# Cross-attention on a context taken relative to its last token: one subtraction in place of the last-key, last-weight and last-value work

## The chip, the core and the metric

The kernel runs on one core of a Trainium2 chip. The metric is the device time of one execution in microseconds, the median of several runs. Engines in what follows: PE is TensorE (matmuls, PEld its weight loads), DVE is VectorE, ACT is ScalarE, POOL is GpSimd, SP is SyncE, which here only issues DMAs.

## The reference, cut to what matters

```python
x = x + cross_attention(layernorm(x), ctx)      # x: (128, 32, 256); ctx: (128, 257, 256)
x = x + self_attention(layernorm(x))            # RMS norm, rotary, sigmoid weights
x = x + expert_ffn(layernorm(x))                # 8 experts, capacity 160, top 1

def cross_attention(query, ctx):                # 16 heads of 16
    q, k, v = query @ Wq.T + bq, ctx @ Wk.T + bk, ctx @ Wv.T + bv
    attn = softmax(einsum('bhnd,bhmd->bhnm', q, k), axis=-1)    # over 257 keys
    return einsum('bhnm,bhmd->bhnd', attn, v) @ Wo.T + bo
```

The context has 257 tokens, one more than two times 128. Everything the change touches is about that last token.

## The kernel before

128 batches of 32 query rows are worked through in 32 tiles of 4 batches (128 rows). The five engine programs are written out by hand, each as a list of instructions with waits on semaphores. `tiles(body)` runs `body(i)` for i = 0 to 33: iteration i does the cross-attention of tile i (for j = 0 to 3, its four batches), the tail of cross-attention and the front of self-attention of tile i-1 (`t1`, active when `s1`), and the rest of self-attention and the routing of tile i-2 (`t2`, active when `s2`). Keys and values are made one batch ahead, so at j = 3 they belong to tile i+1 (`q` says that there is one). The experts follow after the tiles. Since each engine executes its list strictly in order, what stands in front of an instruction in its list matters as much as what it waits for.

Per batch, in the cross-attention: SP loads the transposed context, two batches at a time, into `ctxT[:, r]`; ACT rounds one batch of it to the high part (`context_hi`, L755), POOL subtracts that from the original for the low part (`context_lo`, L1273); PE makes keys (L401) and values (L411) from the two parts in three passes; ACT moves them out (L748, L761). PE makes scores (L428, 257 columns), DVE takes the maxima (`maxima`, L963), ACT the exponentials (`exps`, L739), DVE the normalised weights (`normalise`, L970 and L974), PE transposes 256 of the 257 weights (L444), and after they are copied out (L980, L768, L770) PE multiplies them with 256 values into `gather` (L459).

The 257th token goes another way. In the prologue PE computes all last keys and last values of the 128 batches at once (`last_rows`, L364 to L378). Per batch POOL copies the last key beside the 256 others (`last_key`, L1268) and spreads the last weight over a diagonal (`last_prob`, L1291). Per tile PE multiplies that with a 0/1 matrix (`last_probs`, L470) to bring the last weights to the rows of the output; DVE multiplies them with the last values (`last_values`, L999); ACT takes the even heads of `gather` (`even_heads`, L720), DVE adds the odd heads (`extract`, L985) and then the last-value product and the bias (`attended`, L992). PE then projects it (`project_out`, L477).

Short pieces of PE work of tiles i-1 and i-2 stand in the dictionary `between` at places (j, place) between scores, keys, values, transposes and weighted values of batch j. They share one PSUM bank, `shared`; `turn(name, count)` makes the next user wait until the last reader of the bank is done. At j = 0 before the change: last weights (0,0), cumulative counts and the scores of self-attention `scores2` L515 (0,1), `project_out` (0,2).

Around the turn of an iteration, DVE's list runs: at j = 3 `choose(t2)` (L1114 to L1126, small operations on 8 columns), the statistics `norm_x` (L936 to L947), then at j = 0 `extract(t1)` and `maxima(i, 0)`. POOL's list runs at j = 3: `context_lo(i+1, 1)`, a power for `norm_x`, `residual_bias2`, then `residual_bias` at j = 0. At j = 2 POOL's list runs: `rope_sin`, `last_prob`, `context_lo(i+1, 0)`, and a power (L1263) for the second layer norm, whose result DVE needs in L1102. ACT's list at j = 0 runs: even heads, exponentials, keys, `sigmoid_tanh` (L781, and L782, the reader that frees `shared` for `project_out`), values, `context_hi`.

Of the kernel before, what the change touches and what calls it, by code (L numbers as in the profile page):

```python
# [85 lines left out]
def build(nc, a, out):  # L86
    ctx = ExitStack()
    with ctx:
# [6 lines left out]
        def sem(name):  # L95
# [26 lines left out]
        klast = sb("klast", [P, C, B])  # L122
# [11 lines left out]
        plast = sb("plast", [P, MT, TB, L])  # L134
        att, alast = sb("att", [P, C, P]), sb("alast", [P, C, P])
# [55 lines left out]
        names = """const_in wq_in wkv_in weights_in bf_consts scaled zeroed klast_done vlast_done last_ps  # L191
            xq_in xr_in xn_stat xn_pow xn_done qt_ps xnT_done q_ps qT_done bq_done
            k_done k_evac klast_cp v_done v_evac s_done max_done exp_done rsum_done norm_done plast_done
            pt_done pta_evac ptb_evac pv_done ll_ps ext_step att_done
# [4 lines left out]
            slot_step slot_done sent slots_init slots_zero away_done top_done att_tmp  # L199
# [162 lines left out]
        def _(pe):  # L362
            mm = nc.tensor.matmul

            def last_rows():

                pe.wait_ge(s["wk_in"], 16 * 4)
                pe.wait_ge(s["wv_in"], 16)
                pe.wait_ge(s["wkv_in"], 16 * 6)
                for c in range(C):  # L370
                    for n in range(C):
                        mm(shared[:, c * P:(c + 1) * P], wk[:, n, c * P:(c + 1) * P], lastT[:, n, :],
                           start=n == 0, stop=n == C - 1)
                for c in range(C):
                    for n in range(C):
                        last = mm(shared[:, (C + c) * P:(C + c + 1) * P], wv[:, n, c * P:(c + 1) * P], lastT[:, n, :],
                                  start=n == 0, stop=n == C - 1)
                last.then_inc(s["last_ps"], 1)  # L378
# [36 lines left out]
            def scores(t, j, half):  # L415
                b = TB * t + j
                pe.wait_ge(s["qT_done"], t + 1)
                pe.wait_ge(s["klast_cp"], b + 1)
# [46 lines left out]
            def last_probs(t):  # L465

                pe.wait_ge(s["plast_done"], TB * (t + 1))
                for c in range(C):
                    for g in range(2):
                        last = mm(sh_c[:, c], k["spread"][:, g * P:(g + 1) * P],  # L470
                                  plast[:, 2 * c + g, :, :].rearrange("p j q -> p (j q)"), start=g == 0, stop=g == 1)
                last.then_inc(s["ll_ps"], 1)

            def project_out(x, w, ready, t, done):
                pe.wait_ge(s[ready], t + 1)
# [94 lines left out]
            turn("vlast_done", 1)  # L570
            last_rows()
# [4 lines left out]
            def body(i, half):  # L576
# [15 lines left out]
                    (2, 2): s2 and (lambda: (turn("x2_step", 3 * t2 + 1), project_out(att2, ao, "att2_done", t2, "o2_ps"))),  # L592
# [107 lines left out]
        def _(act):  # L700
# [4 lines left out]
            for dst, src, done in ((wv[:], a["Wv"], "wv_in"), (lastT[:], a["lastT"], "wkv_in")):  # L705
                act.dma_start(dst, src.rearrange("(c p) n -> p c n", c=C)).then_inc(s[done], 16)
# [25 lines left out]
            def exps(t, j):  # L732
                b = TB * t + j
                act.wait_ge(s["plast_done"], b)
# [81 lines left out]
            act.wait_ge(s["wkv_in"], 16 * 6)  # L816
            context_hi(0, 0)
            act.wait_ge(s["last_ps"], 1)
            for c in range(C):
                last = af(klast[:, c, :], shared[:, c * P:(c + 1) * P], ACT.Identity, bias=b_k[:, c:c + 1], scale=1.0)  # L820
            last.then_inc(s["klast_done"], 1)
            context_hi(0, 1)
            keys(0, 0)
# [82 lines left out]
        def _(dve):  # L906
# [59 lines left out]
            def normalise(t, j):  # L966
                b = TB * t + j
                for c in range(C):
# [13 lines left out]
            def extract(t):  # L982

                dve.wait_ge(s["ext_step"], 2 * t + 1)
                v.scalar_tensor_tensor(att[:, :, :], gather[:, :, 1, :], k["odd"], att[:, :, :], ALU.mult, ALU.add  # L985
                                       ).then_inc(s["ext_step"], 1)
            def attended(t):

                dve.wait_ge(s["att_tmp"], t + 1)
                dve.wait_ge(s["ext_step"], 2 * t + 2)  # L990
                for c in range(C):
                    last = v.scalar_tensor_tensor(att[:, c, :], alast[:, c, :], b_v[:, c:c + 1], att[:, c, :],  # L992
                                                  ALU.add, ALU.add)
                last.then_inc(s["att_done"], 1)

            def last_values(t):

                dve.wait_ge(s["ll_ps"], t + 1)
                v.tensor_tensor(alast[:, :, :].rearrange("p c (j q) -> p (c j) q", j=TB),  # L999
                                shared[:, 0:C * P].rearrange("p (x q) -> p x q", q=L),  # L1000
                                vlast[:, bass.ds(t, 1), :, :].rearrange("p a c j -> p (a c j)").unsqueeze(2)
                                .to_broadcast([P, C * TB, L]), ALU.mult).then_inc(s["att_tmp"], 1)
# [136 lines left out]
            for h, heads in ((0, "even"), (1, "odd")):  # L1139
# [5 lines left out]
            dve.wait_ge(s["klast_done"], 1)  # L1145
            v.tensor_copy(vlast[:, :, :, :].rearrange("p t c j -> p c t j"),
                          shared[:, C * P:2 * C * P].rearrange("p (c t j) -> p c t j", c=C, j=TB)).then_inc(s["vlast_done"], 1)

            def body(i, half):
                q, xa, s1, s2 = stages(i)  # L1150
                t1, t2 = i - 1, i - 2
                for j in range(TB):
# [6 lines left out]
                    if j == 0 and s1:  # L1159
                        last_values(t1)  # L1160
# [10 lines left out]
                    if j == 0:  # L1171
                        if s1:
                            attended(t1)
                        if q:
                            norm_x_apply(i + 1)
# [33 lines left out]
                    if once(i):  # L1209
                        setup(j)  # L1210

# [45 lines left out]
        def _(pool):  # L1257
# [7 lines left out]
            def last_key(t, j):  # L1265
                b = TB * t + j
                pool.wait_ge(s["s_done"], floor0(2 * (b - 1)))
                g.tensor_copy(kT[:, j % 2, :, SM:S], klast[:, :, bass.ds(b, 1)]).then_inc(s["klast_cp"], 1)  # L1268
# [16 lines left out]

            def last_prob(t, j):
                b = TB * t + j
                pool.wait_ge(s["norm_done"], 2 * b + 2)
                if j == 0:
                    pool.wait_ge(s["ll_ps"], t)  # L1290
                g.tensor_tensor(plast[:, :, j, :], k["diag"].unsqueeze(1).to_broadcast([P, MT, L]),  # L1291
# [143 lines left out]
```

## Time and profile before

| | us |
|---|---|
| median of 3 runs | 1346.71 (1345.29 to 1346.93) |
| the profiled execution | 1344.86, of which the span from first to last instruction is 1343.0 |
| PE, busy | 1157.5 (86%) |
| DVE, busy | 945.0 (70%) |
| ACT, busy | 872.4 (65%) |
| POOL, busy | 569.7 (42%) |

The profile is of one execution; its engines are seen as rows with a start, a duration, and the idle time before them with what ended it. Durations of neighbouring instructions on an engine overlap a little, since each is reported from its issue to its last write. The tile loop fills the time to about 1187 us, the experts and their loads the rest.

### The profile page before, as it was taken

What the parts mean: (1) busy time and instruction counts of PE and PEld (TensorE: products, weight loads), DVE (VectorE), ACT (ScalarE), POOL (GpSimd) and SP (SyncE); (2) the same over time, 40 slices, a digit from 0 to 9 for tenths busy, and PEclk for the clock granted to TensorE, in tenths of its full rate; (3) what the DMA queues carried; (4) which work ended last, traced back from release to release, by engine and by line L of the source; (5) the groups of instructions that cost most, each with busy time, mean ns of one, the idle gap of its engine ahead of it and who ended that gap; (6) DMA issues with size and microseconds to landing.
All of it is one profiled execution on the core that took longest, in us unless ns stands there. A gap on an engine that the chain in (4) does not pass through costs nothing.

```text
span 1343.0 us, 37302 instructions
## 1 busy us (share of the span) xinstructions
PE 1157.5 (86%) x14033; PEld 936.5 (70%) x14033; DVE 945.0 (70%) x2523; ACT 872.4 (65%) x2443; POOL 569.7 (42%) x1045
## 2 busy tenths in 40 slices
PE   6898889888888898889888888988898888864797
PEld 5676777767767777777767767767777677742697
DVE  3667777777777777777777777877777777763121
ACT  3676767777777667767777777667677777632131
POOL 1244454455444444444454444444444554431121
PEclk9899999999999999999999999999999999975899
DMA  6414211111211111111111111111111111000474
GB/s 148 126 47 144 84 57 43 51 54 51 52 40 45 49 52 47 50 47 39 46 48 50 49 30 50 49 49 46 50 40 39 48 48 45 14 9 13 115 225 153
DMA packets 71904, 81.93 MB, mean 61 GB/s; under 512 B 16987, under 2 KB 50732, under 8 KB 71728
## 3 DMA queue, kind: packets, MB, share of 16 engines
q1 hardware_dynamic: 65280, 75.19, 19.3%
q0 software_dynamic: 3200, 3.71, 0.8%
q8 instruction: 113, 1.85, 0.6%
q10 hardware_dynamic: 3248, 0.66, 0.2%
q14 instruction: 63, 0.52, 0.1%
HBM read 64.79 MB, written 16.56 MB: 61 GB/s over the span
## 4 chain that ended last, share of the span: by engine, by line
DVE 33%; PE 31%; ACT 20%; issue 9%; POOL 6%; SPq 0%; DVEq 0%; DMA 0%; ACTq 0%; POOLq 0%
ACT prob L739 8%; ACT wbd L799 4%; PE score L444 4%; PE vps L411 4%; PE kps L401 4%; DVE prob L974 4%; ACT qz L728 3%; DVE nmx L963 3%; PE shared L477 3%; PE shared L532 3%; PE shared L523 3%; PE score L670 3%; PE score L684 3%; DVE pr L1116 3%; POOL ctx_p L1273 2%
## 5 line engine op out<-in xcount | busy, mean ns | idle before, releaser
L739 ACT ACTIVATE prob<-score,nmx 128x257 f32<-128x257 f32 x512 | 236.2, 476 | 175.8 <-DVE nmx L963 175.0
L401 PE MATMUL kps<-ctx_p,wk_p 128*128 128x256 f32 x1536 | 213.6, 289 | 0.2 <-POOL ctx_p L1273 0.2
L411 PE MATMUL vps<-wv_p,ctx_p 128*128 128x256 f32 x1536 | 212.7, 288 | 0.0
L1273 POOL TENSOR_TENSOR ctx_p<-ctxT,ctx_p 128x512 fp32r<-128x512 f32 x128 | 152.1, 1188 | 119.8 <-ACT ctx_p L755 119.8
L411 PEld LDWEIGHTS vps<-wv_p,ctx_p 128*128 128x128 f32 x1536 | 192.6, 192 | 12.4 <-issue 12.4
L401 PEld LDWEIGHTS kps<-ctx_p,wk_p 128*128 128x128 f32 x1536 | 195.4, 192 | 5.4 <-issue 2.3
L963 DVE TENSOR_REDUCE nmx<-score 128x2 f32<-128x514 f32 x256 | 163.1, 679 | 15.7 <-PE score L428 15.7
L1291 POOL TENSOR_TENSOR plast<-const,prob 128x128 f32<-128x128 f32 x128 | 64.1, 501 | 257.7 <-DVE prob L974 257.7
L974 DVE TENSOR_SCALAR prob<-prob,rsum 128x257 f32<-128x257 f32 x512 | 158.3, 352 | 9.0
L444 PE MATMUL score<-const,prob 128*128 128x128 f32 x1024 | 145.7, 280 | 7.5 <-DVE prob L974 3.5
L444 PEld LDWEIGHTS score<-const,prob 128*128 128x128 f32 x1024 | 114.1, 142 | 44.4 <-DVE prob L974 28.6
L748 ACT ACTIVATE kT<-kps,b_k 128x256 f32<-128x256 f32 x256 | 109.0, 489 | 1.9 <-PE kps L401 1.0
L739 ACT ACTIVATION_READ_ACCUMULATOR prob<-score,nmx 128x1 f32 x512 | 105.2, 205 | 0.0
L459 PE MATMUL gather<-probT,vv 128*32 128x64 f32 x4096 | 90.0, 224 | 11.4 <-DVE probT L980 7.2
L459 PEld LDWEIGHTS gather<-probT,vv 128*32 128x32 f32 x4096 | 72.8, 109 | 34.9 <-issue 21.4
L770 ACT ACTIVATE probT<-score 128x512 f32<-128x512 f32 x128 | 76.9, 601 | 25.8 <-PE score L444 21.8
L428 PE MATMUL score<-kT,qz 32*64 32x257 f32 x2048 | 88.8, 402 | 0.0
L761 ACT ACTIVATE vv<-vps 128x512 f32<-128x512 f32 x128 | 76.0, 594 | 15.9 <-PE vps L411 15.9
L970 DVE RECIPROCAL rsum<-esum 128x2 f32<-128x2 f32 x256 | 41.8, 163 | 63.2 <-ACT prob L739 54.1
L1308 POOL TENSOR_TENSOR qks<-qk,const 128x256 f32<-128x256 f32 x32 | 43.6, 1362 | 100.4 <-DVE qk L1030 100.4
L755 ACT ACTIVATE ctx_p<-ctxT 128x512 fp32r<-128x512 f32 x128 | 80.6, 630 | 0.0
L1263 POOL TENSOR_TENSOR rstd<-ve,const 128x1 f32<-128x1 f32 x64 | 51.2, 799 | 58.5 <-DVE ve L1019 41.3
(163 smaller groups left out, 2188.4 us busy)
## 6 DMA issues: line engine op xcount, KB each, us to landing
ctxT<-in_ctxT SPq DMA_DIRECT2D x128, 257.0 KB, 3.0
w<-in_w SPq DMA_DIRECT2D x16, 1024.0 KB, 9.7
xq<-in_x SPq DMA_DIRECT2D x32, 128.0 KB, 3.3
xr<-in_x SPq DMA_DIRECT2D x32, 128.0 KB, 2.5
qbd<-qkT SPq DMA_DIRECT2D x256, 16.0 KB, 1.8
out<-row SPq DMA_DIRECT2D x32, 128.0 KB, 1.9
slots<-row SPq DMA_DIRECT2D x10, 257.0 KB, 5.6
x_a<-slots SPq DMA_DIRECT2D x8, 129.0 KB, 2.1
```

Of the source, the lines that this page charges most:

```text
L401: last = mm(kps[:, c, :], wk_p[:, x, n, c * P:(c + 1) * P], ctx_p[:, g, y, n, :], start=(n, x) == (0, LO), stop=(n, y) == (C - 1, LO))
L411: last = mm(vps[:, c, :], ctx_p[:, g, x, n, c * P:(c + 1) * P], wv_p[:, y, n, :], start=(n, x) == (0, LO), stop=(n, y) == (C - 1, LO))
L428: last = mm(score[64 * e:64 * e + 64, m, 0:S], qz[rows, half, e, j, :, :].rearrange("p h q -> p (h q)"), kT[rows, b_slot(j), e, :], start= ...
L444: last = nc.tensor.transpose(score[:, 2 * c, at:at + P], prob[:, 2 * c + g, n * P:(n + 1) * P], k["ident"])
L459: last = mm(gather[32 * g:32 * g + 32, c, :, j * L:(j + 1) * L], vv[:, b_slot(j), n, c * P + 32 * g:c * P + 32 * g + 32], probT[:, c, n, 2 ...
L739: last = af(prob[:, m, :], score[:, m, 0:S], ACT.Exp, bias=nmx[:, m:m + 1], scale=1.0, accum_out=esum[:, m:m + 1])
L748: last = af(kT[:, j % 2, c, 0:SM], kps[:, c, :], ACT.Identity, bias=b_k[:, c:c + 1], scale=1.0)
L755: af(ctx_p[:, g, HI, :, :], ctxT[:, r, :, g, 0:SM], ACT.Copy).then_inc(s["ctx_hi"], 1)
L770: af(probT[:, 1, :, :].rearrange("p n x -> p (n x)"), score[:, 2, :], ACT.Copy).then_inc(s["ptb_evac"], 1)
L963: v.tensor_reduce(nmx[:, 2 * c:2 * c + 2], score[:, 2 * c:2 * c + 2, 0:S], AX.X, ALU.max, negate=True).then_inc(s["max_done"], 1)
L974: last = v.tensor_scalar(prob[:, m, :], prob[:, m, :], rsum[:, m:m + 1], None, ALU.mult)
L1273: g.tensor_tensor(ctx_p[:, g_, LO, :, :], ctxT[:, r, :, g_, 0:SM], ctx_p[:, g_, HI, :, :].bitcast(F32), ALU.subtract).then_inc(s["ctx_part ...
```

## The change

Softmax weights sum to one, so subtracting the last token from all tokens of a batch changes the output of attention only by the last token's value, which is added back with weight one; in the scores it changes every key of a row by the same amount, which the softmax ignores. The last token itself becomes zero: its key is the bias alone, its value zero.

- POOL gets `context_sub(t, r)`: one subtraction in place over two batches of `ctxT[:, r]` (1024 columns), after `context_lo` at j = 1 (r = 0 of tile i+1) and at j = 3 (r = 1 of tile i+1). `context_hi` waits for it.
- POOL loses `last_key` and `last_prob`, DVE loses `last_values(t)` and `attended`, PE loses `last_probs`, ACT loses the even heads of cross-attention.
- `extract` has two DVE operations: even heads plus `vlast` (which now holds the last value with its bias), then the odd heads.
- `normalise` covers 256 columns instead of 257. The 257th score is still computed, against a key column written once.
- `last_rows` makes only last values, and moves from the prologue to place (0, 2) of iteration 0.
- In `between`, `scores2` moves to (0, 0) and `positions` is alone at (0, 1).

```diff
@@ tensor
-            turn("vlast_done", 1)
-            last_rows()
@@
-                    (0, 0): s1 and (lambda: (turn("att_tmp", t1 + 1), last_probs(t1))),
-                    (0, 1): lambda: (t3 is not None and positions(t3),
-                                     s2 and (turn("relu_done", t2 + 1), scores2(t2))),
-                    (0, 2): s1 and (lambda: (turn("x1_step", 3 * t1 + 1), project_out(att, wo, "att_done", t1, "o1_ps"))),
+                    (0, 0): s2 and (lambda: (turn("relu_done", t2 + 1), scores2(t2))),
+                    (0, 1): t3 is not None and (lambda: positions(t3)),
+                    (0, 2): (s1 and (lambda: (turn("x1_step", 3 * t1 + 1),
+                                              project_out(att, wo, "ext_step", 2 * t1 + 2, t1, "o1_ps")))
+                             or once(i) and (lambda: (turn("vlast_done", C), last_rows()))),
@@ scalar
-                act.wait_ge(ctx_in[r], 16 * C * (t + 1))
+                act.wait_ge(s["ctx_sub"], 2 * t + r + 1)
@@
-                    if j == 0 and s1:
-                        act.wait_ge(s["o1_ps"], t1)
-                        even_heads(att, gather[:, :, 0, :], "pv_done", TB * (t1 + 1), "ext_step")
@@ vector
-                        last = v.tensor_scalar(prob[:, m, :], prob[:, m, :], rsum[:, m:m + 1], None, ALU.mult)
+                        last = v.tensor_scalar(prob[:, m, 0:SM], prob[:, m, 0:SM], rsum[:, m:m + 1], None, ALU.mult)
@@ extract
+                dve.wait_ge(s["pv_done"], TB * (t + 1))
+                dve.wait_ge(s["o1_ps"], t)
+                if once(t):
+                    dve.wait_ge(s["vlast_done"], C)
+                v.scalar_tensor_tensor(att[:, :, :].rearrange("p c (j q) -> p c j q", j=TB),
+                                       gather[:, :, 0, :].rearrange("p c (j q) -> p c j q", j=TB), k["even"],
+                                       vlast[:, t, :, :].unsqueeze(3).to_broadcast([P, C, TB, L]), ALU.mult, ALU.add
+                                       ).then_inc(s["ext_step"], 1)
                 dve.wait_ge(s["ext_step"], 2 * t + 1)
                 v.scalar_tensor_tensor(att[:, :, :], gather[:, :, 1, :], k["odd"], att[:, :, :], ALU.mult, ALU.add
                                        ).then_inc(s["ext_step"], 1)
-            def attended(t):
...
-            def last_values(t):
...
+            def last_values():
+                dve.wait_ge(s["last_ps"], 1)
+                for c in range(C):
+                    v.tensor_scalar(vlast[:, :, c, :], sh_c[:, c].rearrange("p (t j) -> p t j", j=TB), b_v[:, c:c + 1], None,
+                                    ALU.add).then_inc(s["vlast_done"], 1)
@@ gpsimd
+            def context_sub(t, r):
+
+                b = TB * t + 2 * r
+                pool.wait_ge(ctx_in[r], 16 * C * (t + 1))
+                if t == 0 and r == 0:
+                    pool.wait_ge(s["last_in"], 16)
+                g.tensor_tensor(ctxT[:, r, :, :, 0:SM], ctxT[:, r, :, :, 0:SM],
+                                lastT[:, :, b:b + 2].unsqueeze(3).to_broadcast([P, C, 2, SM]), ALU.subtract
+                                ).then_inc(s["ctx_sub"], 1)
@@ body of gpsimd
-                    if xa and (j < TB - 1 or q):
-                        last_key(*((i, j + 1) if j < TB - 1 else (i + 1, 0)))
...
-                    if xa:
-                        last_prob(i, j)
...
                     if xa and (j < 2 or q):
                         context_lo(*((i, j + 2) if j < 2 else (i + 1, j - 2)))
+                    if q and j % 2:
+                        context_sub(i + 1, j // 2)
```

## Rows read from the trace of the kernel before

**Rows 1.** The page's first line.

```profile
span 1343.0 us, 37302 instructions
```

**Rows 2.** Chain that ended last, in order of time: start us, us, engine, tile, line.

```profile
599.82 1.18 DVE pr L1116
...
607.67 1.10 PE shared L477 x4
...
617.00 1.10 PE shared L523 x16
...
628.41 1.15 POOL ctx_p L1273
...
630.69 0.41 PE shared L483 x2
```

**Rows 3.** Timeline (start us, us, engine, line) around an iteration's turn; L1116's min/median/max.

```profile
599.78 1.18 POOL L1273 TENSOR_TENSOR ctx_p<-ctxT,ctx_p 128x512 fp32r<-128x512 f32 x1 [1.83 <-ACT ctx_p L755]
601.22 0.23 DVE L1120 SCALAR_TENSOR_TENSOR eqr<-pr,row,const 128x8 f32<-128x8 f32 x1
602.67 0.48 DVE L985 SCALAR_TENSOR_TENSOR att<-gather,const,att 128x256 f32<-128x256 f32 x1
603.06 1.28 DVE L963 TENSOR_REDUCE nmx<-score 128x2 f32<-128x514 f32 x2
...
1187.45 0.23 DVE L1116 TENSOR_SCALAR pr<-ex,rse 128x8 f32<-128x8 f32 x1
...
L1116 DVE TENSOR_SCALAR pr<-ex,rse x32: 230/1163/1175, 122.1 to 1240.6; 128x8 f32<-128x8 f32 x32
```

**Rows 4.** Timeline, iteration 0: POOL beside DVE operations with two SBUF inputs.

```profile
53.41 1.74 POOL L1273 TENSOR_TENSOR ctx_p<-ctxT,ctx_p 128x512 fp32r<-128x512 f32 x1 [1.46 <-ACT ctx_p L755]
54.03 1.67 DVE L957 TENSOR_TENSOR av_p<-av,av_p 128x512 fp32r<-128x512 f32 x1
```

**Rows 5.** Groups by line: busy us, mean ns of one, idle before.

```profile
L974 DVE TENSOR_SCALAR prob<-prob,rsum 128x257 f32<-128x257 f32 x512 | 158.3, 352 | 9.0
L1273 POOL TENSOR_TENSOR ctx_p<-ctxT,ctx_p 128x512 fp32r<-128x512 f32 x128 | 152.1, 1188 | 119.8 <-ACT ctx_p L755 119.8
L1296 POOL TENSOR_TENSOR xr<-xr,r_o 128x256 f32<-128x256 f32 x32 | 23.3, 727 | 0.0
L925 DVE TENSOR_SCALAR aqk<-aqk,qn 128x256 f32<-128x256 f32 x2 | 0.7, 343 | 0.0
```

**Rows 6.** Timeline of PE and ACT at j = 0 of one iteration.

```profile
600.48 1.16 PE L470 MATMUL shared<-plast,const 128*128 128x128 f32 x8
604.73 1.07 PE L515 MATMUL shared<-qbd,qkT 128*32 128x256 f32 x16 [1.14 <-DVE alast L999]
607.67 1.10 PE L477 MATMUL shared<-wo,att 128*128 128x256 f32 x4 [0.25 <-DVE att L992]
...
606.85 0.64 ACT L782 ACTIVATE sneg<-shared 128x512 f32<-128x512 f32 x1
```

**Rows 7.** Timeline of ACT and DVE at j = 2 of the same iteration.

```profile
626.49 0.62 ACT L755 ACTIVATE ctx_p<-ctxT 128x512 fp32r<-128x512 f32 x1
...
626.93 0.62 DVE L974 TENSOR_SCALAR prob<-prob,rsum 128x257 f32<-128x257 f32 x2
627.46 0.68 DVE L1041 TENSOR_TENSOR qk<-qkc,qks 128x512 f32<-128x512 f32 x1
629.31 0.15 DVE L1098 TENSOR_SCALAR ve<-mv 128x1 f32<-128x1 f32 x1
```

**Rows 8.** Timeline of POOL and DVE at j = 1 of the same iteration.

```profile
619.99 1.18 POOL L1273 TENSOR_TENSOR ctx_p<-ctxT,ctx_p 128x512 fp32r<-128x512 f32 x1
...
623.30 0.42 DVE L1079 TENSOR_TENSOR att<-att,ssum 128x256 f32<-128x256 f32 x1
```

**Rows 9.** Stretches: us, busy us of PE, PEld, DVE, ACT, POOL; PEclk, DMA share, GB/s.

```profile
36.00:40.00 4.00, 2.37 (x50) 1.28 (x42) 0.75 (x5) 1.87 (x5) 1.31 (x2) 0.61 0.09 16
...
603.40:607.60 4.20, 2.88 (x30) 2.00 (x30) 3.82 (x15) 3.76 (x13) 1.90 (x4) 1.00 0.24 64
```

More of the change, by code:

```diff
@@ L133, in build @@
         probT = sb("probT", [P, C, 2, HH * L])
-        plast = sb("plast", [P, MT, TB, L])
-        att, alast = sb("att", [P, C, P]), sb("alast", [P, C, P])
+        att = sb("att", [P, C, P])
         xr, x1, x1b, y1, sq = (sb(n, [P, D]) for n in ("xr", "x1", "x1b", "y1", "sq"))
@@ L365, in last_rows @@
             def last_rows():
-                pe.wait_ge(s["wk_in"], 16 * 4)
                 pe.wait_ge(s["wv_in"], 16)
-                pe.wait_ge(s["wkv_in"], 16 * 6)
+                pe.wait_ge(s["last_in"], 16)
                 for c in range(C):
                     for n in range(C):
[L372 to L377, printed above, removed]
+                        last = mm(sh_c[:, c], wv[:, n, c * P:(c + 1) * P], lastT[:, n, :], start=n == 0, stop=n == C - 1)
                 last.then_inc(s["last_ps"], 1)
@@ L417, in scores @@
                 pe.wait_ge(s["qT_done"], t + 1)
-                pe.wait_ge(s["klast_cp"], b + 1)
+                if b == 0:
+                    pe.wait_ge(s["bk_done"], 1)
                 pe.wait_ge(s["k_evac"], b + 1)
@@ L463, in weighted_values, with project_out @@
                 last.then_inc(s["pv_done"], 1)
[L465 to L475, printed above, removed]
+            def project_out(x, w, ready, count, t, done):
+                pe.wait_ge(s[ready], count)
                 for c in range(C):
@@ L591, in body @@
                     (2, 0): s1 and (lambda: (turn("qk_done", t1 + 1), project_qk(t1))),
-                    (2, 2): s2 and (lambda: (turn("x2_step", 3 * t2 + 1), project_out(att2, ao, "att2_done", t2, "o2_ps"))),
+                    (2, 2): s2 and (lambda: (turn("x2_step", 3 * t2 + 1), project_out(att2, ao, "att2_done", t2 + 1, t2, "o2_ps"))),
                     (2, 3): s1 and (lambda: (turn("qkT_done", t1 + 1), transpose_qk(t1))),
@@ L704, in _ @@
             load_paired(act, wk, a["Wk"], "wk_in")
-            for dst, src, done in ((wv[:], a["Wv"], "wv_in"), (lastT[:], a["lastT"], "wkv_in")):
+            for dst, src, done in ((lastT[:], a["lastT"], "last_in"), (wv[:], a["Wv"], "wv_in")):
                 act.dma_start(dst, src.rearrange("(c p) n -> p c n", c=C)).then_inc(s[done], 16)
@@ L733, in exps @@
                 b = TB * t + j
-                act.wait_ge(s["plast_done"], b)
                 for c in range(C):
@@ L815, in _ @@
             queries(0, 0)
-            act.wait_ge(s["wkv_in"], 16 * 6)
             context_hi(0, 0)
[L818 to L821, printed above, removed]
             context_hi(0, 1)
+            act.wait_ge(s["wkv_in"], 16 * 5)
             keys(0, 0)
@@ L1144, in _ @@
             weight_lo(wv_p[:, LO], wv[:, :, :], wv_p[:, HI], 2)
-            dve.wait_ge(s["klast_done"], 1)
-            v.tensor_copy(vlast[:, :, :, :].rearrange("p t c j -> p c t j"),
-                          shared[:, C * P:2 * C * P].rearrange("p (c t j) -> p c t j", c=C, j=TB)).then_inc(s["vlast_done"], 1)
+            dve.wait_ge(s["wkv_in"], 16 * 5)
+            v.tensor_copy(kT[:, :, :, SM:S], b_k[:, :].unsqueeze(1).unsqueeze(3).to_broadcast([P, 2, C, 1])
+                          ).then_inc(s["bk_done"], 1)
             def body(i, half):
@@ L1158, in body @@
                         norm_x(1)
-                    if j == 0 and s1:
-                        last_values(t1)
                     if j == 1 and s1:
@@ L1170, in body @@
                         position(t2 - 1)
[L1171 to L1175, printed above, removed]
+                    if j == 0 and q:
+                        norm_x_apply(i + 1)
                     if j == 3 and s2:
@@ L1210, in body @@
                         setup(j)
+                    if j == 0 and once(i):
+                        last_values()
             tiles(body)
@@ L1284, in rows_parts @@
                                 ).then_inc(s["y1T_parts"], 1)
[L1286 to L1291, printed above, removed]
-                                prob[:, :, SM:S].to_broadcast([P, MT, L]), ALU.mult).then_inc(s["plast_done"], 1)
             def residual_bias(t):
@@ L1354, in _ @@
             power("q", "xn_stat", 3, 0, "xn_pow")
+            context_sub(0, 0)
             context_lo(0, 0)
             context_lo(0, 1)
-            pool.wait_ge(s["klast_done"], 1)
-            last_key(0, 0)
+            context_sub(0, 1)
             def body(i, half):
```

23 lines of the change are left out of this document (4 added, 19 removed).

## The prediction, made before the changed kernel was run

> **What bounds the kernel now.** PE is busy for 86% of the span [rows 1], which suggests that less PE work means less time. I don't go by that share, since it is an average; I read the chain that ended last, in order of time, over one whole iteration. The pattern repeats with a period of 36.7 us (L1116 starts at 599.82 and, 16 iterations on, at 1187.45 [rows 2, 3]), so what one iteration gains or loses counts about 30 times. The chain runs through DVE, ACT, PE and POOL in turn [rows 2]: DVE's small operations at the turn of the iteration (L1116), the first projection (L477 at 607.67), then DVE, ACT and at 617.00 the weight sums (L523), a stretch of PE, then at j = 2 DVE and POOL (L1273 at 628.41), the transpose of the normed rows (L483 at 630.69), and PE until the next turn. The reader is to see two places at which PE stands and waits for DVE: before L477, and before L483.
>
> The first place, backwards, from the timelines: L477 starts at 607.67, its row says that `att` from L992 came last, but L782, which frees the PSUM bank, ends at 606.85 + 0.64 = 607.49, only 0.12 to 0.18 us earlier [rows 6]. Both hang on the exponentials, these on the maxima L963, which start at 603.06 [rows 3] although PE finished these scores before 600.6 (L470, the next on PE, has started at 600.48 [rows 6]). So DVE is late: it works without a pause through L1116, L1120, the statistics, L985 and then L963 [rows 3]. And in that row of work one instruction is odd. L1116 handles 8 columns and takes 1.16 to 1.18 us in 29 of 32 iterations, 0.23 us in the last three; the first of these three is at 1187.45, where no context is prepared [rows 3]. In the 29 cases it lies beside POOL's L1273, which starts at 599.78 and ends at 600.96; L1116 ends at 599.82 + 1.17 = 600.99 [rows 2, 3]. The DVE instruction is held until the POOL instruction ends.
>
> **The same for other pairs.** In iteration 0 an L1273 beside two-input DVE subtractions takes 1.74 instead of 1.19 us, and the DVE subtraction that comes up behind it takes 1.67 us and ends at 55.70, 0.55 us after POOL's end at 55.15 [rows 4, 5]. So a DVE operation with two SBUF inputs is held as well, and when the holder ends, the one who waited goes next, even if the other engine has more to do. The Trainium skill states it as a rule (SBUF — State Buffer, section Who interferes with whom): GpSimd and a VectorE instruction that is in a two-port mode or has two SBUF inputs exclude each other for the whole instruction. The trace agrees with its L1116 and L957 rows; the rule speaks against this change, since it makes long POOL instructions expensive to DVE.
>
> **Part A: `context_sub` at j = 3.** It is one POOL instruction of 1024 columns; the trace has none. Bounds: twice L1273 (512 columns, 1.19 us) is 2.38 us; by the slope from 256 columns (L1296, 0.727) to 512, 1.80 ns a column, it is 1.188 + 512 x 0.0018 = 2.11 us [rows 5]. I take 2.2. It stands directly behind `context_lo(i+1, 1)`, so it starts at about 600.96 in the frame of these rows, and ends at about 603.15. L1116 has waited and goes first; then L1120, which has two SBUF inputs (`pr` and the constant), comes up at 601.22 [rows 3] and is held until about 603.2 to 603.4, instead of ending at 601.45. That is +1.65 to +1.95 us. If POOL kept its turn instead, L1116 itself would be held 2.1 to 2.4 us longer. Less than zero is excluded, since nothing that DVE does here gets shorter. I take +1.9 us. Behind L1120 wait all of DVE's next steps, and for them the exponentials, the keys' and the bank's reader on ACT, and L477. Times 29 iterations (those with `choose` and a next tile): 29 x 1.9 = +55 us.
>
> **Part B: the first operation of `extract`.** The even heads move from ACT, which is idle there, to DVE in front of the maxima. From L985, the same size, 602.67 to the next start 603.06, it is 0.39 us [rows 3]. L477 now waits for L782 (607.49) and no longer for L992, which gives back the 0.12 us of 607.67 - 607.55 [rows 6], so +0.27 us. Times 31: +8 us. The other DVE savings of j = 0 (`last_values`, `attended`, about 1.1 us) lie behind the maxima; they end at L992, which is off the path now, and DVE waits for L477 afterwards. They bring nothing more.
>
> **Part C: `context_lo` at j = 2 without `last_prob` ahead of it.** Before, POOL waited for the normalised weights to build `last_prob`, then came L1273 at 628.41 [rows 2]. Now only the high part, ready at 626.49 + 0.62 = 627.11, holds it [rows 7], and it starts at about 627.19, in the middle of the two L974 (626.93 to 627.55) and ahead of L1041 (627.46) [rows 7]. Either it slips between the two L974 and the second one ends at about 628.43 instead of 627.55 (+0.88), or it waits for the second and L1041, two SBUF inputs, ends 0.55 us after it, at about 629.2 instead of 628.14 (+1.0). Is L974 of the kind that is held? It takes 352 ns for 257 columns, as L925 takes 343 for 256 [rows 5], and L925 is the same form; none of the 512 L974 was ever beside a long POOL instruction, so the trace has no row of one held. The lower bound is then a small gain: L1098 ends at 629.46 [rows 7] and POOL's power came at 629.56, right behind L1273 (628.41 + 1.15) [rows 2], so 0.1 us is there to gain if nothing is held. I take +0.9 us: after L1041 come the residual, L1098, the power, L1102 and L483, for which PE waits. Times 30: +27 us.
>
> A side result from the same rows: 256 columns in place of 257 in `normalise` changes nothing that counts [rows 5]. The Trainium skill (VectorE: DVE Perf Modes, section Mode 2×_2P) has the two-port mode for an even outer dimension or for an odd one equal in source and destination, so by it 257 ran in that mode already; a step to twice the speed at 256 would be some 134 ns of the 352 (an estimate from that page's clock and rates), and 4 x 128 of those some 69 us of DVE time. The row speaks for the first reading, and the sum goes without it.
>
> **Part D: what is removed from PE.** `last_probs` takes 1.16 us at 600.48, and L515 waits 1.14 us for `last_values` behind it [rows 6]. Both go, 2.3 us of PE time in an iteration. But keys, `scores2` and values then only end earlier in front of the same wait of L477, which hangs on DVE and ACT. I cost the gain at zero; the cover is that wait, and the gain shows up as a longer idle time before L477, some 2.3 + 2.2 us divided over the waits of `positions` (for the extract) and L477.
>
> **Part E: the rest.** `context_sub` at j = 1 follows L1273, which moves up by about 0.4 us as `last_prob` is gone: it would end about 620.8 + 2.2 = 623.0, ahead of L1079 at 623.30 [rows 8], which has two SBUF inputs. Between 0 and +0.3 us an iteration; I take 0. The two loads of SP and their waits hang on the same `context_lo` as before, and the sums are done long before `context_hi` asks. `scores2` earlier at (0,0) still finds its bank free. In the prologue `last_rows` goes from ahead of the first keys (about -1.7 us), but at (0,2) of iteration 0 its reader stands on DVE behind two large memsets, which holds PE's next user of the bank (about +2.5 us). In iteration 32 the chain starts without `last_probs` (about -1.5 us). Together -1 us, with 3 us either way.
>
> **Sum.** 55 + 8 + 27 - 1 = +89 us on the profiled execution's 1344.86: 1434. The median of the runs is 1.85 us above that execution, so 1436. With the ends of the parts (A 1.65 to 2.4, C 0.88 to 1.0, E 0 to 0.3): 1424 to 1465.
>
> **The rivals.**
> 1. *PE sets the pace, and the change is faster.* If the removed PE work and the wait behind it were on the path, 31 x 2.05 to 2.3 us would go: 1346.7 - 67 = about 1280. For it speaks the 86% of PE. Against it, that L477 waits for DVE and ACT after all of that. It decides if the maxima of batch 0 start no later than before, that is, if neither `context_sub` nor the added operation delays DVE. 10%.
> 2. *Only one of the collisions costs.* If `context_lo` at j = 2 falls beside instructions that aren't held: 1346.7 + 55 + 8 - 4 = 1406. If `context_sub` at j = 3 isn't in DVE's way but C is: 1346.7 + 8 + 27 = 1382. Against it, the 29 equal cases of L1116 and the fixed 36.7 us pattern. 17%.
> 3. *Neither costs.* Only B and the 0.1 of C: 1346.7 + 8 - 3 = 1352. 6%.
> 4. *The clock of PE falls in the longer wait.* In 603.4 to 607.6 PE is busy 2.88 of 4.2 us and granted 1.00 (2.4 GHz); in 36 to 40 it was busy 2.37 of 4.0 us with idle gaps and was granted 0.61, partly 1.2 GHz [rows 9]. In the changed kernel PE would have only the values, some 1.7 us, to do in about 6.5 us before L477. If the clock falls each time and PE's next work, which has about 1.2 us of slack before L523, is stretched, I take +0.5 to +1.5 us an iteration, 1450 to 1480, middle 1466. 12%.
>
> **How the numbers follow.** My forecast, both collisions with the clock up, has 55%: 1436, of its own range 1424 to 1465. The range must leave out no more than 2 in 10: I leave out rivals 1 and 3 (16%) and reach from below the lower case of rival 2 to beyond rival 4's middle: 1375 to 1475. A measurement can tell about 0.2%, 2.7 us, from no change. Faster: rival 1, 10%, and a chance in rival 3 of a little less, 1%. Same: 3%, from rival 3. Slower: 86%.
>
> **What would show it.** In the profile after: L1120 or L1116 with a median of about 2 us (part A right), and the maxima of batch 0 some 2.3 us later behind `choose`; L974 or L1041 at j = 2 lengthened by about 0.9 us (C right); a period of 39.8 us; PE idle for over 4 us in j = 0; DVE busier although it has less to do. If L1120 is 0.23 us and L477 starts about 5 us after the turn, I am wrong about the path, and rival 1 holds. If POOL's `context_sub` is itself lengthened and DVE isn't, who is held was the other way round.

## The result: slower by 8.8%, and the profile after

| | before | after |
|---|---|---|
| median, us | 1346.15 (4 runs) | 1463.13 (4 runs, 1462.67 to 1467.35) |
| ratio, 95% interval | | 1.088 [1.086, 1.090] |
| profiled execution | 1344.86 | 1463.35 |
| PE granted clock, mean | 0.970 | 0.916 |

PE, DVE and ACT run fewer instructions than before (PE 13,769 for 14,033), and the time is up by 117 us. The page of after, its first line, three engine groups (busy us, mean ns of one) and the min/median/max of the instruction that the prediction called L1120 (now L1093):

```profile
span 1461.5 us, 36200 instructions
...
L949 DVE TENSOR_SCALAR prob<-prob,rsum 128x256 f32<-128x256 f32 x512 | 188.5, 410 | 9.0
L1241 POOL TENSOR_TENSOR ctxT<-ctxT,lastT 128x1024 f32<-128x1024 f32 x64 | 121.9, 1904 | 4.1 <-DMA ctxT<-in_ctxT 4.1
L461 PE MATMUL shared<-wo,att 128*128 128x256 f32 x128 | 58.6, 605 | 46.2 <-ACT sneg L764 45.5
...
L1093 DVE SCALAR_TENSOR_TENSOR eqr<-pr,row,const x32: 227/1620/1623, 126.1 to 1358.7; 128x8 f32<-128x8 f32 x32
```

The normalised weights (before 352 ns for 257 columns [rows 5]) take 410 ns for 256 on average: 29 of the 512 take about 1.32 us, most of the others 0.35 us as before. A matmul of the projection L461 takes 605 ns on average, a mix of two kinds: the four of an iteration together take 1.13 us in some iterations and 2.07 us in most (below). An operation on 8 columns has a median of 1.62 us, against 0.23 in [rows 3]. The timeline of POOL and DVE at the turn of an iteration (start us, us, engine, line), the place of [rows 3]:

```profile
777.03 1.19 POOL L1248 TENSOR_TENSOR ctx_p<-ctxT,ctx_p 128x512 fp32r<-128x512 f32 x1 [6.53 <-ACT ctx_p L737]
778.17 1.90 POOL L1241 TENSOR_TENSOR ctxT<-ctxT,lastT 128x1024 f32<-128x1024 f32 x1
...
777.08 1.17 DVE L1089 TENSOR_SCALAR pr<-ex,rse 128x8 f32<-128x8 f32 x1
778.28 0.16 DVE L1091 TENSOR_REDUCE row<-pr 128x1 f32<-128x8 f32 x1
778.47 1.62 DVE L1093 SCALAR_TENSOR_TENSOR eqr<-pr,row,const 128x8 f32<-128x8 f32 x1
...
781.33 0.48 DVE L963 SCALAR_TENSOR_TENSOR att<-gather,const,vlast 128x256 f32<-128x256 f32 x1
781.85 0.48 DVE L968 SCALAR_TENSOR_TENSOR att<-gather,const,att 128x256 f32<-128x256 f32 x1
782.25 1.28 DVE L938 TENSOR_REDUCE nmx<-score 128x2 f32<-128x514 f32 x2
```

L1089 ends when `context_lo` does, as before. Then the subtraction runs from 778.17 to 780.07, and L1093, issued at 778.47, ends at 780.09: held to its end. L1091, a reduction with one input that runs beside the same subtraction, takes its usual 0.16 us. From the start of this small-operation row to the maxima it is 782.25 - 777.08 = 5.17 us, against 603.06 - 599.82 = 3.24 in [rows 3]: +1.93, of it 1.39 the held L1093 and 0.53 the second operation of `extract`.

At j = 2, the place of [rows 7], DVE and POOL:

```profile
765.64 0.62 DVE L949 TENSOR_SCALAR prob<-prob,rsum 128x256 f32<-128x256 f32 x2
766.37 1.59 DVE L949 TENSOR_SCALAR prob<-prob,rsum 128x256 f32<-128x256 f32 x2
767.88 0.68 DVE L1014 TENSOR_TENSOR qk<-qkc,qks 128x512 f32<-128x512 f32 x1
...
766.63 1.18 POOL L1248 TENSOR_TENSOR ctx_p<-ctxT,ctx_p 128x512 fp32r<-128x512 f32 x1 [1.38 <-ACT ctx_p L737]
```

`context_lo` has slipped between the two L949 of a pair, which takes 1.59 in place of 0.62 us. And PE at j = 0, in four iterations (the bracket is the idle time before the first matmul):

```profile
782.59 0.17 PE L534 MATMUL gather<-oh,tri_bf 128*128 128x8 bf16 x1 [2.15 <-DVE att L968]
786.66 1.13 PE L461 MATMUL shared<-wo,att 128*128 128x256 f32 x4 [2.35 <-ACT sneg L764]
...
826.14 2.08 PE L461 MATMUL shared<-wo,att 128*128 128x256 f32 x4 [1.26 <-ACT sneg L764]
...
908.02 2.07 PE L461 MATMUL shared<-wo,att 128*128 128x256 f32 x4 [1.30 <-ACT sneg L764]
...
948.97 2.07 PE L461 MATMUL shared<-wo,att 128*128 128x256 f32 x4 [1.31 <-ACT sneg L764]
```

PE stands for 2.15 us ahead of the positions and for 2.35 us ahead of L461, in place of 1.14 and 0.25 in [rows 6]. With L461 still at full clock the iteration takes 826.14 - 786.66 = 39.48 us, before 36.7. But in most iterations L461 takes 2.07 us for its four matmuls, and the iteration 948.97 - 908.02 = 40.95. The stretches around 948.97 say why (us; busy us of PE, PEld, DVE, ACT, POOL; granted clock, DMA share, GB/s):

```profile
940.00:945.00 5.00, 2.84 (x39) 2.03 (x31) 4.65 (x11) 0.00 (x0) 3.59 (x5) 1.00 0.37 109
945.00:948.95 3.95, 2.67 (x14) 2.37 (x13) 3.02 (x12) 3.67 (x13) 0.73 (x2) 0.52 0.01 2
948.95:952.50 3.55, 3.53 (x14) 2.99 (x14) 0.99 (x2) 1.51 (x4) 1.18 (x1) 0.57 0.00 0
```

After 5 us in which PE was busy for 2.84, the granted clock is 0.52 and 0.57, nearly all of it 1.2 GHz, over the values and over L461 and the transposes behind it. Closer in, with the row of PE for the positions:

```profile
944.90 0.17 PE L534 MATMUL gather<-oh,tri_bf 128*128 128x8 bf16 x1 [2.16 <-DVE att L968]
...
943.00:945.20 2.20, 0.30 (x4) 0.33 (x5) 1.99 (x7) 0.00 (x0) 1.41 (x3) 1.00 0.20 76
945.18:952.01 6.83, 5.52 (x22) 4.76 (x22) 3.33 (x14) 5.17 (x15) 1.73 (x2) 0.50 0.00 1
```

The clock falls at 945.18, 0.28 us behind the end of the wait ahead of the positions, and stays down until 952.01. The idle time ahead of L461 comes when it is already down. Of the 24 falls between 120 and 1150 us, 23 come within 1.5 us of the end of that first wait.

So 117 us are about 30 x 2.74 = 82 us of a longer iteration at full clock, and 35 us of clock. These are the two theories that the experiments had to hold apart, with the three parts of the first.

### The profile page after: what moved, and what is told of

Its sections match the earlier page's. It is cut to its first block, busy times and chain, and to the rows that moved or that the text cites. A ratio compares the mean times of both kernels' runs of the same rounds, so it can differ in the third digit from the quotient of the medians.

```text
span 1461.5 us, 36200 instructions
## 1 busy us (share of the span) xinstructions
PE 1187.5 (81%) x13769; PEld 956.8 (65%) x13769; DVE 1004.0 (69%) x2461; ACT 854.2 (58%) x2409; POOL 594.7 (41%) x853
## 4 chain that ended last, share of the span: by engine, by line
DVE 37%; PE 31%; ACT 21%; issue 8%; POOL 1%; SPq 1%; DMA 0%; DVEq 0%; ACTq 0%; POOLq 0%
ACT prob L721 7%; PE score L437 5%; ACT wbd L781 4%; PE shared L461 4%; DVE prob L949 4%; PE vps L403 3%; PE kps L393 3%; DVE eqr L1093 3%; DVE nmx L938 3%; ACT qz L711 3%; PE score L653 3%; PE shared L516 3%; PE shared L507 3%; PE score L667 2%; DVE pr L1089 2%
## 5 line engine op out<-in xcount | busy, mean ns | idle before, releaser
L403 PE MATMUL vps<-wv_p,ctx_p 128*128 128x256 f32 x1536 | 235.3, 308 | 0.0
L403 PEld LDWEIGHTS vps<-wv_p,ctx_p 128*128 128x128 f32 x1536 | 213.7, 211 | 0.0
L949 DVE TENSOR_SCALAR prob<-prob,rsum 128x256 f32<-128x256 f32 x512 | 188.5, 410 | 9.0
L437 PE MATMUL score<-const,prob 128*128 128x128 f32 x1024 | 160.8, 300 | 35.6 <-DVE prob L949 33.5
L437 PEld LDWEIGHTS score<-const,prob 128*128 128x128 f32 x1024 | 130.7, 156 | 76.7 <-DVE prob L949 56.9
L1241 POOL TENSOR_TENSOR ctxT<-ctxT,lastT 128x1024 f32<-128x1024 f32 x64 | 121.9, 1904 | 4.1 <-DMA ctxT<-in_ctxT 4.1
L1233 POOL TENSOR_TENSOR rstd<-ve,const 128x1 f32<-128x1 f32 x64 | 38.9, 607 | 154.1 <-DVE ve L1071 79.5
L452 PE MATMUL gather<-probT,vv 128*32 128x64 f32 x4096 | 94.2, 226 | 6.0 <-DVE probT L955 1.8
L461 PE MATMUL shared<-wo,att 128*128 128x256 f32 x128 | 58.6, 605 | 46.2 <-ACT sneg L764 45.5
L955 DVE COPY probT<-score 128x512 f32<-128x512 f32 x96 | 66.1, 688 | 27.0 <-PE score L437 26.9
```

Of the source, the lines that this page charges most:

```text
L403: last = mm(vps[:, c, :], ctx_p[:, g, x, n, c * P:(c + 1) * P], wv_p[:, y, n, :], start=(n, x) == (0, LO), stop=(n, y) == (C - 1, LO))
L437: last = nc.tensor.transpose(score[:, 2 * c, at:at + P], prob[:, 2 * c + g, n * P:(n + 1) * P], k["ident"])
L452: last = mm(gather[32 * g:32 * g + 32, c, :, j * L:(j + 1) * L], vv[:, b_slot(j), n, c * P + 32 * g:c * P + 32 * g + 32], probT[:, c, n, 2 ...
L949: last = v.tensor_scalar(prob[:, m, 0:SM], prob[:, m, 0:SM], rsum[:, m:m + 1], None, ALU.mult)
L1241: g.tensor_tensor(ctxT[:, r, :, :, 0:SM], ctxT[:, r, :, :, 0:SM], lastT[:, :, b:b + 2].unsqueeze(3).to_broadcast([P, C, 2, SM]), ALU.subtr ...
```

## The experiments

Beside each median stands the period read from the starts of the first projection in iterations at full clock, since the clock adds a varying amount. Runs x1 to x4, x5 to x8 and x9 to x12 shared their runs of the kernel before (medians 1346.65, 1344.45 and 1345.99).

**x1, the subtraction at j = 3 made short.** It leaves most of the context of batches 2 and 3 unsubtracted.

```diff
+                w = 8 if r else SM
-                g.tensor_tensor(ctxT[:, r, :, :, 0:SM], ctxT[:, r, :, :, 0:SM], ...
+                g.tensor_tensor(ctxT[:, r, :, :, 0:w], ctxT[:, r, :, :, 0:w], ...
```

> The subtraction at j = 3 (r = 1) covers 8 of 256 columns per batch and chunk, so batches 2 and 3 of each tile keep most of their context unshifted; everything else as in the changed kernel. Theory (GpSimd's 1.90 us instruction holds DVE's L1093 for 1.39 us, and PE's longer wait then brings the clock down): L1093 back to 0.23 us, the period of an iteration with the clock up from 39.5 to 38.1 us, and the granted clock falls less often; 1387 us if it stays up, 1424 if it still falls in every iteration. Rival (the time comes from the clock or from the order of PE's work, the held instruction is a symptom): within 10 us of 1463.

Measured: 1407.58 us, ratio 1.044 [1.042, 1.046]; median of L1093 227 ns; period 38.1 us. Two starts, the time between them 38.10:

```profile
755.42 1.13 PE L461 MATMUL shared<-wo,att 128*128 128x256 f32 x4 [2.35 <-ACT sneg L764]
793.52 1.13 PE L461 MATMUL shared<-wo,att 128*128 128x256 f32 x4 [2.35 <-ACT sneg L764]
```

The held instruction costs 1.4 us an iteration, 40 us in all; 15 more came back from the clock.

**x2, `context_lo` at j = 2 held until the weights are normalised.**

```diff
+                    if xa and j == 2 and q:
+                        pool.wait_ge(s["norm_done"], 2 * (TB * i + 2) + 2)
                     if xa and (j < 2 or q):
                         context_lo(...)
```

> GpSimd waits for both normalised halves of batch 2 before context_lo at j = 2, as the removed last_prob made it do; nothing else changes. Theory (context_lo slips between the two L949 and holds the second for 0.97 us, and all after it is late by that): the second pair of L949 back to 0.62 us, period 0.95 us shorter in all 30 iterations, 1434 us, the clock still falling at j = 0. Rival (the delay at j = 2 is covered by other waits): L949 shorter, time within 5 us of 1463.

Measured: 1427.54 us, 1.059 [1.057, 1.062]; the longest L949 is 0.83 instead of 1.33 us; period 38.48 us (767.78 to 806.26), 1.0 less. As expected, with 6 us more from the clock. A wait that was removed with `last_prob` is put back, and the kernel is 36 us faster.

**x3, both operations of `extract` behind the maxima.**

```diff
-                    if j == 0 and s1:
-                        extract(t1)
                     if xa:
                         maxima(i, j)
+                    if j == 0 and s1:
+                        extract(t1)
```

> Both operations of extract stand behind the maxima of batch 0 on DVE instead of ahead of them. Theory (DVE's row of work ahead of the maxima sets the time of L461): 0.92 us less ahead of the maxima, 0.92 us an iteration, 1436 us, or down to 1400 if the shorter wait keeps the clock up. Rival (L461 is then held by the positions or by att instead): 1450 to 1463.

Measured: 1461.32 us, 1.086 [1.084, 1.088]. The time did not move, though the few iterations at full clock take 38.48 us (948.30 to 986.78), 1.0 less than after. The expectation in time failed. The timeline of PE at j = 0 shows where the gain went:

```profile
781.77 0.17 PE L534 MATMUL gather<-oh,tri_bf 128*128 128x8 bf16 x1 [3.38 <-DVE att L968]
781.82 2.91 PE L403 MATMUL vps<-wv_p,ctx_p 128*128 128x256 f32 x12
784.53 1.91 PE L461 MATMUL shared<-wo,att 128*128 128x256 f32 x4
```

PE now waits 3.38 us ahead of the positions, which need `extract`; the clock has fallen, the values take 2.91 instead of 1.67 us, and L461 has no idle time ahead of it: PE at 1.2 GHz, not ACT, is what is late. What DVE gained, the clock took.

**x4, the kernel before with one idle subtraction added.**

```diff
+                    if q and j == 3:
+                        pool.wait_ge(s["extra_done"], i + 1)
+                        g.tensor_tensor(extra[:, :, :, :], extra[:, :, :, :],
+                                        lastT[:, :, 0:2].unsqueeze(3).to_broadcast([P, C, 2, SM]), ALU.subtract
+                                        ).then_inc(s["extra_done"], 1)
```

> The kernel before, with one thing added: a GpSimd subtraction of 1024 columns on a tile that nobody reads, at j = 3 behind context_lo(i+1, 1). Theory: L1120 (0.23 us) becomes 1.62 us, the maxima of batch 0 come 1.4 us later, 29 times, 1346 + 40 = 1386 us, up to 1420 if the clock falls as well. Rival (a GpSimd instruction alone costs nothing, it is the waiting for the subtracted context that does): 1346 to 1350.

Measured: 1418.42 us, 1.053 [1.051, 1.055], 72 us for an instruction whose result nobody reads. Its timeline at the turn:

```profile
672.15 1.90 POOL L1384 TENSOR_TENSOR extra<-extra,lastT 128x1024 f32<-128x1024 f32 x1
...
672.45 1.62 DVE L1121 SCALAR_TENSOR_TENSOR eqr<-pr,row,const 128x8 f32<-128x8 f32 x1
```

The same 1.62 us, in the kernel without any other part of the change. Periods go from 38.07 (721.85 to 759.92) up to 40.1: +1.3 us for the hold, the rest the clock, which falls here in most iterations though no wait of PE is longer than 1.8 us. Waiting for the subtracted context is thereby out as a cause of this part.

**x5 and x9, unneeded matmuls in PE's waits.** x5 computes the next batch's values once more ahead of the positions, x9 does so again behind them. The edit shown is that of x9; x5 has only the first `values_again`.

```diff
-                    (0, 1): t3 is not None and (lambda: positions(t3)),
+                    (0, 1): t3 is not None and (lambda: (xa and values_again(i, 1), positions(t3),
+                                                         xa and values_again(i, 1))),
```

> The changed kernel with PE work that nobody needs: the values of the next batch are computed twice at (0,1), the first time (12 matmuls, about 1.6 us) in the 2.15 us for which PE waits ahead of the positions. Theory (what is left over the period of 39.5 us is the clock, which falls because PE has too little to do in j = 0): the clock stays up, all periods 39.5 us, 1346.6 + 30 x 2.74 = 1429 us although PE does more. Rival (the iterations of 41 us have another cause, or more PE work costs time): 1463 us or more.

Measured for x5: 1463.12 us, 1.088 [1.087, 1.090]: nothing gained. The wait ahead of the positions is down to 0.7 us, but the one of 2.35 us right ahead of the projection is still there, and the projection (here L470) is still at 1.2 GHz in 22 iterations:

```profile
866.97 2.07 PE L470 MATMUL shared<-wo,att 128*128 128x256 f32 x4 [2.35 <-ACT sneg L773]
```

The fall has only moved: it comes at the end of the wait of 2.35 us, for the row above at 866.63, and the projection runs through it. The mean clock rose to 0.943, over the values, where it is worth nothing. So x5 did not decide; x9 closed the second gap too.

> As the first filler run, with the unneeded values computed once more behind the positions: 24 unneeded matmuls in an iteration, 3.2 us, so that PE is idle for only about 1.3 us of j = 0 in place of 4.5. The first filler left the 2.35 us wait right ahead of L461 as it was, and L461 still ran at 1.2 GHz. Theory (the low clock there is the second cost): the clock stays up, L461 1.13 us, all periods 39.5 us, 1345.5 + 30 x 2.74 = 1428 us. Rival (the 41 us iterations have another cause, or the filler delays the values): 1463 us or more.

Measured for x9: 1424.97 us, 1.058 [1.056, 1.060], 38 us faster than after, with 24 matmuls more in each iteration. PE at j = 0, and a whole iteration's stretch:

```profile
920.89 0.17 PE L543 MATMUL gather<-oh,tri_bf 128*128 128x8 bf16 x1 [0.72 <-DVE att L978]
924.97 1.13 PE L470 MATMUL shared<-wo,att 128*128 128x256 f32 x4 [0.91 <-ACT sneg L774]
...
900.00:939.50 39.50, 34.66 (x437) 28.25 (x436) 30.53 (x76) 25.90 (x73) 18.45 (x27) 1.00 0.15 42
```

The clock stays at 1.00 through the tiles, the periods are 39.5 us (a few up to 39.8), and the time is 3 us from the expectation. That settles the split of the 117 us: about 79 for DVE, 38 for the clock.

**x10, late extract with the double filler.**

> The late extract together with the double filler. The late extract alone brought its period with the clock up to 38.46 us but the time stayed at 1461. Theory (that gain was eaten by the clock falling for longer): with the clock held up, 1345.5 + 30 x 1.73 = 1397 us. Rival (the late extract gains nothing): as the double filler alone.

Measured: 1465.43 us, 1.089 [1.087, 1.091]. Neither theory's number. PE waits 1.89 us for `extract` ahead of the positions, the clock falls there (at 786.44, behind the wait that ends at 785.45), and the unneeded matmuls then run partly at 1.2 GHz themselves: the two sets of values take 2.16 and 2.66 us, and the projection follows without idle time, late. This run says nothing on the late extract.

**x6, the subtraction moved within j = 3.** It runs after the normed rows, beside DVE's maxima (in one iteration from 700.40 to 702.30, the maxima from 700.28 to 701.57, with no DVE instruction lengthened).

```diff
-                    if q and j % 2:
-                        context_sub(i + 1, j // 2)
+                    if q and j == 1:
+                        context_sub(i + 1, 0)
@@ ahead of context_lo
+                    if q and j == 3:
+                        if s2:
+                            pool.wait_ge(s["y2_done"], t2 + 1)
+                        context_sub(i + 1, 1)
```

> The changed kernel with the subtraction of batches 2 and 3 moved: ahead of context_lo(i+1, 1) at j = 3, behind the normed rows, where DVE runs the maxima of batch 3, which have one input in PSUM. All work stays. Theory: L1093 0.23 us, period with the clock up 38.1 us, as with the short subtraction; 1388 us, or up to 1408 with the clock. Rival (the subtraction costs by its mere length on GpSimd): 1440 to 1463.

Measured: 1404.43 us, 1.045 [1.042, 1.049]; L1093 227 ns; period 38.07 (714.53 less 676.45 is 38.08). The full subtraction costs no more in the right place than the short one did.

**x7, all three: x2, x3 and x6 together.**

> Subtraction moved, context_lo at j = 2 held until the weights are normalised, extract behind the maxima: all three parts undone at once, nothing of the change taken back. Theory (the parts add up in the period with the clock up): 39.47 - 1.40 - 0.99 - 1.01 = 36.07 us, less than the 36.73 before; 1326 us with the clock up, 1360 to 1386 if it falls as often as in the single runs. Rival (another wait comes in below 36.7 us): 1346 or more with a period over 36.7.

Measured: 1360.64 us, 1.013 [1.011, 1.014]. The shortest periods are 36.2 us, as the three parts add up; most are 37.5, with the clock down again around the projection (2.07 us), behind a wait of 1.95 us ahead of the positions. It is still slower than before; at full clock, by the periods (36.2 against 36.73), it would not be.

**x8, x7 and one more: `context_lo(i+1, 1)` after `choose`.** This takes away the hold of L1089 (L1116 before), which the kernel before had already.

```diff
+                    if xa and j == 3 and q and s2:
+                        pool.wait_ge(s["oh_done"], t2 + 1)
```

> As the run before, and context_lo(i+1, 1) waits until choose is done, so that it doesn't hold L1089 either, as it did with L1116 in the kernel before (1.16 instead of 0.23 us). Theory: 0.93 us less again, period 35.1 us with the clock up, 1297 us, or up to 1350 with the clock falling. Rival (DVE no longer sets the pace, PE or ACT does): period 35.6 to 36.1.

Measured: 1300.19 us, 0.967 [0.965, 0.969] of the kernel before: faster than both. L1089's min/median/max, two starts, and an iteration's stretch:

```profile
L1089 DVE TENSOR_SCALAR pr<-ex,rse x32: 229/231/233, 121.1 to 1195.2; 128x8 f32<-128x8 f32 x32
...
585.81 1.13 PE L461 MATMUL shared<-wo,att 128*128 128x256 f32 x4 [0.24 <-ACT sneg L764]
621.04 1.13 PE L461 MATMUL shared<-wo,att 128*128 128x256 f32 x4 [0.23 <-ACT sneg L764]
...
590.00:625.20 35.20, 31.81 (x414) 25.36 (x414) 27.08 (x76) 25.78 (x74) 18.91 (x27) 1.00 0.17 49
```

Period 35.23 us, wait ahead of L461 0.24 us, clock 1.00 from 76 to 1140 us, nearly to the end of the tiles: with DVE on time, the wait ahead of the positions is 0.21 us and the clock doesn't fall, so both terms go at once.

**x11, that last wait alone, in the kernel before.**

> The kernel before, with one wait added: context_lo(i+1, 1) on GpSimd starts only when choose is done on DVE. Theory: L1116 0.23 instead of 1.16 us, 29 times 0.93 us, period 35.8 us, 1319 us; what the four-part version (1300 us) gains beyond that belongs to the removed last-token work. Rival (the kernel before is held by something else as well): 1340 or more.

Measured: 1318.40 us, 0.979 [0.978, 0.981]; period 35.80. One added wait is worth 28 us. So of the 44 us by which x8 beats its own runs of the kernel before, 28 belong to this wait; 16 are left (by the periods, 35.80 less 35.23, about 17) for the removed work together with the later `extract`, which this run does not tell apart.

**x12, a memset in place of x4's subtraction.** Timed once.

> The kernel before, with a GpSimd memset of 1024 columns, which reads nothing from SBUF, where the earlier run had the subtraction. Theory by two-input operations being held only for reads: L1120 (two SBUF inputs) stays at 0.23 us and L1126 (one input, written in a two-port mode) is held until the memset ends, if it lasts over 0.8 us. Rival (any GpSimd instruction holds both): L1120 is the one that is lengthened. The time is 1346 to 1375 us.

Measured: 1378.28 us, above the expected range. Neither theory: the operation ahead of both was held.

```profile
653.23 1.18 POOL L1274 TENSOR_TENSOR ctx_p<-ctxT,ctx_p 128x512 fp32r<-128x512 f32 x1 [1.83 <-ACT ctx_p L756]
653.28 2.06 DVE L1117 TENSOR_SCALAR pr<-ex,rse 128x8 f32<-128x8 f32 x1
654.35 0.95 POOL L1384 MEMSET extra<- 128x1024 f32 x1
655.57 0.23 DVE L1121 SCALAR_TENSOR_TENSOR eqr<-pr,row,const 128x8 f32<-128x8 f32 x1
```

The waiting DVE instruction did not get its turn between the two POOL instructions, but only after the memset, at 655.30; with a subtraction second it did. Whether two-input operations are held by an instruction that reads nothing stays open, since none ran beside the memset.

## Why the prediction was right, and where not

The direction, the bound and the mechanisms held: 1463 lies in the range 1375 to 1475, which was made to reach beyond rival 4's middle. The forecast itself, 1436, is 27 us low, and that 1463 still lies at the end of its own range, 1424 to 1465, is luck: that end came from a part A of up to 2.4 us, which measured 1.39. The case that happened is the forecast's parts *and* rival 4 (1450 to 1480, middle 1466), to which I gave 12%; the forecast as told (both collisions, clock up) is x9's 1425 us, not the changed kernel.

- *What bounds the kernel.* Right. DVE's row of work ahead of the maxima sets the time of the projection: x1, x4 and x6 move it by what L1093 is held. Rival 1, PE by its 86%, fell: after has less PE work and x9 more, and the time goes the other way. Rivals 2 and 3 fell with it, since both collisions cost (x6 and x2).
- *Part A, 1.9 us.* The mechanism was right, to the instruction and to the turn-taking (L1089 first, then the subtraction, then L1093 held). That whoever waited goes next held for a subtraction behind `context_lo`, but not for a memset (x12), so it is no general rule. The size was off: 1.39 us. The subtraction takes 1.90 us and not 2.2, below both of my bounds, 2.11 and 2.38: from 512 to 1024 columns it is 1.39 ns a column, not the 1.8 of the step from 256 to 512. The rest, about 0.2 us, is for the most part that L1093's own 0.23 us largely runs within the hold (it ends 0.02 us after the subtraction).
- *Part B, +0.27 net.* It was about 0.41: the second operation waits for the first one's result, so they start 0.52 and not 0.39 us apart, and 0.53 us more lie ahead of the maxima, of which I take off the 0.12 that L992 gives back. No run tests it alone; what x6 (1.40) and x2 (1.0) leave of the 2.74 us is 0.34.
- *Part C, +0.9.* Right: 0.97 us on the second L949, 1.0 us in the period by x2. It was the first of my two orders. The question whether L974 can be held is answered by the row of 1.59 us. The small gain of the lower bound, for the case that L974 can't be held, did not come.
- *Sum of A, B and C.* 3.07 us forecast; 2.74 measured (39.47 - 36.73). A was 0.5 us too high, B and C together 0.2 us too low.
- *Part D, nothing for the removed PE work.* Right as a sum, and the longer wait came as forecast (2.15 + 2.35 us). What I called a cover had a price of its own: this wait is what brought the clock down, as x9 shows, which fills it.
- *Part E.* The subtraction at j = 1 costs nothing: L1052, which was L1079, takes 0.42 us. It does not delay `context_hi` either: ACT is never idle ahead of L737.
- *Rival 4.* My step was the size: 0.5 to 1.5 us; measured 40.95 - 39.48 = 1.47 in an iteration, at the upper end, in most iterations, 38 us by x9. The step that failed is its chance. I had the row of the clock falling in gaps [rows 9] and wrote down that PE would have 1.7 us of work in 6.5; from that the fall should have been the likeliest case and not a rival. The slack that I counted on, 1.2 us ahead of the weight sums, does not help, since the slow matmuls are L461 and the transposes, which are themselves on the path: set beside the iteration of 786.66, the one of 908.02 is 0.90 us late when L461 is done and 1.48 us late behind the transposes, and the weight sums (L507) then start 1.48 us later too, with the same 1.19 us of idle time ahead of them.

The Trainium skill's rule (SBUF — State Buffer, section Who interferes with whom) is that whichever of GpSimd and VectorE issues first has the SBUF ports that they share for its whole instruction. By that rule both held instructions wait for the end of the GpSimd one, and the 1.62 and 1.59 us of after agree.

## What to carry to other kernels

Before an instruction is put on GpSimd, look at what VectorE runs beside it: an 8-column operation with two SBUF inputs behind a 1.9 us GpSimd one costs 1.4 us if it is on the path, and the same GpSimd instruction a few places earlier costs nothing (x6). A wait that is removed can have kept two engines apart (x2, 36 us), and one that is added can be worth more than the work taken out (x11, 28 us). And a wait of TensorE is not free cover: price it with the clock down too, and check whether the work behind the wait is on the path.

## What the runs showed of the hardware that I had not expected

- The clock fell at the end of one wait of PE of 2.16 us (after) or 2.35 us (x5), 1.4 us behind one of 1.95 us (x7), and behind two of 1.7 and 1.14 us with 0.2 us of matmuls between them (x4); in six iterations of x12 it did so behind two of 1.2 to 1.3 and 1.1 us. In the kernel before and in x9, with waits of at most 1.19 us, it stayed at 1.00 through the tiles between 100 and 1150 us. In after it cost 1.47 us an iteration, about half of the 2.74 us that DVE's delays cost.
- A DVE instruction held behind one GpSimd subtraction goes next if a second subtraction follows (1.17 us, after and x4), but was held through both when the second was a memset (2.06 us, x12).
- GpSimd's in-place subtraction of 1024 columns takes 1.90 us, 1.6 times the 1.19 us of `context_lo` with 512.
